# Attention scores and maxima of two heads side by side on half the array each, with a new PSUM plan, the causal score mask on GpSimd and straight-line steps

## What is computed

```
x = x + attention_a(layernorm(x))     # causal; three heads weigh a third of the tokens by 1.6
x = x + ffn(layernorm(x))
x = x + attention_b(layernorm(x))     # not causal; q and k are rotated by position
x = x + ffn(layernorm(x))

scores = einsum('bhqd,bhkd->bhqk', q, k) / sqrt(8)
out = einsum('bhqk,bhkd->bhqd', softmax(scores), v) @ w_out + bias
ffn:  h = silu(x @ w1 * s1) * (x @ w2 * s2); h = gelu(h @ h1 * s); h = gelu(h @ h2 * s); out = h @ w3 * s
```

## Time and profile before

| what | value |
|---|---|
| device time, median of 3 runs | 2662.58 us (2661.67 to 2663.25) |
| profiled execution: its span, first to last instruction | 2666.0 us |
| PE busy | 2374.0 us (89%), 15042 matmuls |
| DVE busy | 1745.9 us (65%) |
| ACT busy | 1516.8 us (57%) |
| POOL busy | 825.3 us (31%) |
| attention a, first to last weighted sum | 99.9 to 859.5 us |
| attention b, first to last weighted sum | 1374.9 to 2239.2 us |

### The profile page before, as it was taken

How to read it: one execution, slowest core, us unless ns; L and a number is a source line. 1 busy time by engine, 2 the same in 40 slices (tenths; PEclk the granted TensorE clock), 3 DMA queues, 4 the chain that set the end, 5 groups by cost and what they waited for, 6 DMA issues and landing times. The chain is left out here.

```text
span 2666.0 us, 48309 instructions
## 1 busy us (share of the span) xinstructions
PE 2374.0 (89%) x15042; PEld 1272.8 (48%) x15042; DVE 1745.9 (65%) x2625; ACT 1516.8 (57%) x2948; POOL 825.3 (31%) x933
## 2 busy tenths in 40 slices
PE   1999889889897699999489999999999995899998
PEld 0455445445442488887223323333233321688886
DVE  6766666656661576665198878787777870666663
ACT  0366556556565355555037767676676774455554
POOL 3223222222210255544322222222223300355454
PEclk9899999999998799999589999999999998999999
DMA  5334334334331000000224333332333311000000
GB/s 163 85 80 100 83 74 103 76 74 102 76 76 20 10 0 0 0 0 1 71 51 91 72 74 73 72 86 63 74 71 69 86 35 28 5 12 12 12 12 12
DMA packets 114561, 146.81 MB, mean 55 GB/s; under 512 B 27600, under 2 KB 88656, under 8 KB 113232
## 3 DMA queue, kind: packets, MB, share of 16 engines
q1 hardware_dynamic: 114384, 144.60, 23.6%
HBM read 78.47 MB, written 66.06 MB: 54 GB/s over the span
## 5 line engine op out<-in xcount | busy, mean ns | idle before, releaser
L533 DVE TENSOR_REDUCE b_negmax<-ps_max 128x2 f32<-128x1024 f32 x512 | 610.4, 1219 | 180.8 <-PE ps_max L652 180.6
L617 ACT ACTIVATE b_prob<-ps_score 128x512 f32<-128x512 f32 x1024 | 555.8, 594 | 260.9 <-PE ps_score L636 244.0
L617 ACT ACTIVATE a_prob<-ps_score 128x512 f32<-128x512 f32 (+3 forms) x1024 | 419.5, 435 | 271.9 <-PE ps_score L639 219.8
L533 DVE TENSOR_REDUCE a_negmax<-ps_max 128x2 f32<-128x256 f32 (+3 forms) x512 | 407.4, 820 | 226.9 <-PE ps_max L655 226.4
L652 PE MATMUL ps_max<-stack_k,b_stack_q 96*128 96x512 bf16 x1024 | 383.3, 395 | 33.0 <-DVE b_negmax L533 17.5
L636 PE MATMUL ps_score<-b_stack_q,stack_k 100*128 100x512 bf16 x1024 | 395.5, 389 | 18.5 <-ACT b_prob L617 17.0
L652 PE MATMUL ps_max<-stack_k,a_stack_q 96*128 96x128 bf16 (+3 forms) x1024 | 305.1, 312 | 57.1 <-DVE a_negmax L533 25.5
L636 PE MATMUL ps_score<-a_stack_q,stack_k 100*128 100x512 bf16 (+3 forms) x1024 | 319.3, 314 | 16.0 <-ACT a_prob L617 14.0
L636 PEld LDWEIGHTS ps_score<-b_stack_q,stack_k 100*128 100x128 bf16 x1024 | 99.2, 98 | 383.1 <-ACT b_prob L617 328.0
L670 PE MATMUL ps<-b_prob,b_v_aug 128*9 128x512 f32 x2048 | 272.6, 605 | 8.8 <-ACT b_o_raw L589 7.1
L945 PE MATMUL ps_score<-fb_h,w_hi 128*128 128x512 f32 x1024 | 247.4, 398 | 3.9 <-DVE fb_h L860 2.8
(11 more groups left out here) (142 smaller groups left out, 3116.1 us busy)
## 6 DMA issues: line engine op xcount, KB each, us to landing
stack_k<-d_stack SPq DMA_DIRECT2D x128, 192.0 KB, 4.0
d_stack<-a_parts SPq DMA_DIRECT2D x64, 192.0 KB, 2.8
a_stack_q<-d_stack SPq DMA_DIRECT2D x64, 192.0 KB, 3.3
d_stack<-b_parts SPq DMA_DIRECT2D x64, 192.0 KB, 2.8
b_stack_q<-d_stack SPq DMA_DIRECT2D x64, 192.0 KB, 3.7
d_stack<-a_parts SPq DMA_DIRECT2D x64, 128.0 KB, 2.8
d_stack<-b_parts SPq DMA_DIRECT2D x64, 128.0 KB, 2.8
d_stack<-a_parts SPq DMA_DIRECT2D x64, 64.0 KB, 2.5
```

Of the source, the lines that this page charges most:

```text
L533: dve.tensor_reduce(m["negmax"][:, t, :, p], m["ps_max"][:, 2 * (k % 2):2 * (k % 2) + 2, 0:keys], AX.X, ALU.max, negate=True).then_inc(s[" ...
L617: act.activation(m["prob"][u % 2][:, g, lo:S], m["ps_score"][:, g % 2, 0:S - lo], ACT.Exp)\
```

## The change

Five things change in the attention stages.

1. `stack_q` and `stack_k` hold head 0 of a pair in rows 0 to 49 and head 1 in rows 64 to 113 (`SIDE` = 64): 48 rows of products and 2 of the negated maximum. `stack_k` exists once. A score matmul has 50 contraction rows and a maximum matmul 48; the built program gives each a tile of 64 array rows by 128 columns, and the two heads of a pair stand behind each other on different row halves and write different banks.
2. The score mask matmul is gone. GpSimd instead sets the upper triangle of the diagonal block to zero in `prob` after the Exp (`mask`, line 498, 16 a step, attention a only), and `weigh` waits for it. The mask of the maxima stays on PE.
3. `prob` has 4 buffers in place of 2, and `weigh` comes two units behind its scores in place of one.
4. PSUM is dealt in turns by consumer: what ACT reads (scores, transposed maxima, transposed x) rotates over 3 banks of `ps_score`, what DVE reads (maxima, projections, output projection) over the two double banks of `ps_max`. Each use waits only for the use that had the bank before.
5. All loops in the program text are written out, in the ffn stages too, and GpSimd's work of a step is spread over its units. The reciprocal moves from unit 5 to 7, the transposed maxima of half 0 from unit 12 to 10.

```
-            def step(n, c):
+            for n in range(STEPS):
                 for u in range(UNITS):
-
-                    if on(n, 1):
-                        maxes(n - 1, 1 - c, 2 * u, 0)
-                    if on(n, 2):
-                        score(n - 2, c, u, 0)
...
+                    if on(n, 2):
+                        scores(n, u, 0)
+                    if on(n, 1):
+                        maxes(n, 2 * u)
+                    if u < 2 and on(n, 3):
+                        weigh(n - 3, UNITS - 2 + u)
+                    if u >= 2 and on(n, 2):
+                        weigh(n - 2, u - 2)
+                    if on(n, 2):
+                        scores(n, u, 1)
+                    if on(n, 1):
+                        maxes(n, 2 * u + 1)
                     misc_work(n, u)
```

```
+                for o in range(2):
+                    k = 4 * u + 2 * half + o
+                    rows = slice(SIDE * o, SIDE * o + KROWS + AUG)
+                    act_bank_free(pe, n, "score", k)
+                    pe.matmul(act_bank("score", k)[:, 0:S - lo], m["stack_k"][c][rows, p, P * j:P * (j + 1)],
+                              m["stack_q"][c][rows, p, lo:S], start=True, stop=True).then_inc(s["score"], 1)
...
+                dve_banks_free(pe, n, "max", k)
+                to, keys = dve_banks("max", k), P * (t + 1) if causal else S
+                for o in range(2):
+                    rows = slice(SIDE * o, SIDE * o + KROWS)
+                    last = pe.matmul(to[:, o, 0:keys], m["stack_q"][c][rows, p, P * t:P * (t + 1)],
+                                     m["stack_k"][c][rows, p, 0:keys], start=True, stop=True)
                 if causal:
-                    last = pe.matmul(m["ps_score"][:, g % 2, 0:P], m["mask_k"][:], m["ident_b"][:],
-                                     start=False, stop=True, skip_group_check=True)
...
+                    for o in range(2):
+                        last = pe.matmul(to[:, o, keys - P:keys], m["mask_q"][:], m["ident_b"][:],
+                                         start=False, stop=True, skip_group_check=True)
+                last.then_inc(s["max_ps"], 1)
```

```
+            def mask(b, u):
+
+                pool.wait_ge(s["prob"], count(4 * UNITS, b, 4 * u + 4))
+                at = P * (u % T)
+                tri = m["prob"][u % PROBS][:, :, at:at + P]
+                pool.affine_select(out=tri, in_=tri, compare_op=ALU.is_ge, fill=0.0, base=0,
+                                   pattern=[[0, 4], [1, P]], channel_multiplier=-1).then_inc(s["masked"], 1)
...
+    act_turns, dve_turns = [], []
+    for u in range(UNITS):
+        act_turns += [("score", 2, 4 * u + g) for g in range(4)]
+        dve_turns += [("max", 1, 2 * u), ("max", 1, 2 * u + 1)]
+        for name, lag in (("nm1", 2), ("nm0", 1), ("xT", 0)):
+            if SLOT[name] == u:
+                act_turns.append((name, lag, 0))
+        for name, lag in (("proj", 3), ("q", 0), ("qr", 0), ("k", 0), ("kr", 0), ("v", 0)):
+            if SLOT[name] == u and (rotary or name not in ("qr", "kr")):
+                dve_turns.append((name, lag, 0))
```

More of the change, by code:

```diff
@@ L173, in _ @@
             for c in range(2):
-                last = dve.memset(m["stack_k"][c][:], 0.0)
+                last = dve.memset(m["stack_k"][c][:], 1.0)
             last.then_inc(zeroed, 1)
             dve.wait_ge(zeroed, 1)
[L177 to L182, removed]
         @block.sync
@@ L256, in attention @@
     m["parts"] = sb("parts", [P, 2, 3, S], BF16)
[L257 removed]
+    m["prob"] = [sb(f"prob{c}", [P, 4, S]) for c in range(PROBS)]
     m["negmax"] = sb("negmax", [P, T, 2, PAIRS])
@@ L291, in attention @@
[L291 to L296, removed]
-        while True:
[L298 to L306, removed]
+    def on(n, lag):
+        return 0 <= n - lag < B
@@ new lines, in load @@
+            def load(b, c, h):
+                wait(sp, s["score"], count(4 * UNITS, b - 2, 2 * UNITS * (h + 1)))
+                pairs = slice(HALF * h, HALF * (h + 1))
+                for o in range(2):
+                    q, k = (m["d_stack"][i, o].rearrange("t d p n -> (t d) p n") for i in range(2))
+                    rows = slice(SIDE * o, SIDE * o + KROWS)
+                    sp.dma_start(m["stack_q"][c][rows, pairs, :], q[:, pairs, :]).then_inc(s[f"half{h}"], 16)
+                    sp.dma_start(m["stack_k"][c][rows, pairs, :], k[:, pairs, :]).then_inc(s[f"half{h}"], 16)
@@ L406, in _ @@
                         .then_inc(s["w_raw"], 16)
-            pipeline(sp, step)
+            for n in range(STEPS):
+                c = n % 2
+                if on(n, 2):
+                    aug(1, n - 2, c)
+                if on(n, 3):
+                    outputs(n - 3)
+                if on(n, 0):
+                    store(n)
+                    load(n, c, 0)
+                if on(n, 1):
+                    aug(0, n - 1, 1 - c)
+                if on(n, 0):
+                    load(n, c, 1)
         @block.gpsimd
@@ L589, in group_out @@
                 act.activation(m["o_raw"][:, G], m["ps_out"][:], ACT.Copy).then_inc(s["o_raw"], 1)
-            def step(n, c):
-                if causal and isinstance(n, int) and n == 2:
+            for n in range(STEPS):
+                if causal and n == 2:
                     act.wait_ge(s["w_rest"], len(W_PIECES))
@@ L624, in _, with scores @@
             pe.wait_ge(s["loads"], 80 if rotary else 64)
-            def score(b, c, u, g):
+            def scores(n, u, half):
+                b, c = n - 2, n % 2
                 G, j = u // T, u % T
-                p, o = 2 * G + g // 2, g % 2
-                if g == 0 and u % (UNITS // 2) == 0:
+                p, lo = 2 * G + half, width(j)
+                if half == 0 and u % (UNITS // 2) == 0:
                     h = u // (UNITS // 2)
@@ L783, in pipeline @@
         def pipeline(eng, step):
-            for n in range(3):
-                step(n)
-            with eng.Fori(3, B - 1) as n:
-                step(n)
-            for n in range(B - 1, B + 2):
+            for n in range(B + 2):
                 step(n)
```

443 lines of the change are left out of this document (217 added, 226 removed).

## The result

| | us, median | runs |
|---|---|---|
| before | 2662.9 (2661.7 to 2664.8) | 4 |
| changed | 2573.3 (2562.1 to 2578.8) | 4 |

The ratio is 0.9652, 95% interval 0.9627 to 0.9677: faster by 3.5%. The forecast was 2404 us with a range of 2300 to 2500. The sign was right, but only a third of the forecast gain came, and the time lies outside the range. The profiled execution of the changed kernel took 2562.1 us, the quickest of its four.

The account below looks back on a forecast made before the run. PE was taken to bound attention, afterwards SP's transfers in a and DVE with waits in b. Savings of 143 us in a and 115.5 in b off the 2666.0 us span, less 3.4 to the median, gave 2404 us (range 2300 to 2500).

Parts of the forecast that it names:

- A pair costs what one costs: Attention scores and maxima: two matmuls on two row halves cost one's 0.22 us, saving 14.1 us a step in b.
- Changes of the array's shape cost 0.09 us each: Attention a: about three more shape changes a unit at 0.09 us each add 4.3 us of PE a step.
- TensorE needs 33.9 us of a step of a: Attention a: PE work a step falls from 42.2 to 33.9 us.
- my bounds (37.3): PE work in a step of a: 29.6 us if shape changes cost nothing, 37.3 at 0.16 us each.
- the 36 us that I gave to a step without a ring: Attention a, steps 2 and 16, where SP has no outputs or no stores: 33.9 us and 2 for waits.
- The mask takes 0.65 us and is hidden: GpSimd in attention a: 16 masks of 0.65 us, 10.4 us a step, hidden behind the two units between scores and sums.
- b at 48 us: Attention b: a step takes 48 us, between DVE's 43.9 and the earlier 53.7, with added waits from PE's in-order issue.
- Loop edges go, straight-line code costs nothing: Attention: PE's 3.14 us "issue" idle every second step of a goes; writing out loops, ffn's too, costs nothing.
- That is 39.5 us, above PE's 33.9: Attention a: a step lasts 39.5 us, set by SP's transfers, and PE idles some 4 us.
- the ring of attention a: Landing of half 0, units 0 and 1, `aug` (5.5 us), 33.0 us of transfers, 1 us for unit 7, next landing.
- the sign that I had named: In the new profile, a step of a near 39.5 us whose first maximum waits for a load of `stack_k`.
- The second rival: Attention a at about 44 us a step, PE at 1.2 GHz after its wait, slow units lengthening the ring: 2462 us; 18%.

Follow-up runs that it names:

- the kernel with the cut ring: Changed kernel with the reciprocal at unit 6, half 0's transposed maxima at unit 9, their rows stored before its q and k loads: 2475.8 us.
- The run with the wait filled: Changed kernel with five extra fp32 matmuls ahead of TensorE's wait at the start of each step of attention a from step 2: 2533.2 us, 0.9493.

## Why the prediction was wrong

**The forecast by its steps.**

- *A pair costs what one costs*: right. Pair to pair 0.22 us at clock 1.00, and 0.45 on the same rows.
- *Changes of the array's shape cost 0.09 us each*: borne out for one unit, as a reading of starts. In the rows above the maxima of 128 columns take 0.16 us to the next instruction and their masks 0.21. By the 0.06 us for 128 columns in the earlier trace rows the pair would be 0.06 and the two masks 0.12: 0.10 and 0.09 us more, for a change of shape behind each.
- *TensorE needs 33.9 us of a step of a*: too low by up to 3.3 us. The clean step of the kernel with the cut ring lasts 39.04 us, 37.2 of them busy, which is the upper end of my bounds (37.3). Short waits for the third bank are counted as busy there, and no view tells them apart. So the 36 us that I gave to a step without a ring were too few as well.
- *The mask takes 0.65 us and is hidden*: right on both counts.
- *b at 48 us*: right in size (48.88), and wrong in its floor. I took VectorE's 43.9 us as the bound and added 4 for coupling. With VectorE's load cut by 16 us the step still takes 48.0. Of the waits that I had listed, the one for the third bank of the scores is 2.7 us a step where I had put 1.3, and the one for ScalarE's copy ahead of the first sum 0.7 where I had put 2, by the two rows of waits above.
- *Loop edges go, straight-line code costs nothing*: the edges went: no step of a begins with a wait of the cause "issue". But the rest of the span is 11.6 us longer: 3.1 us in one step of the ffn behind a, 4.7 us in that ffn's last steps, 3.1 us in steps 0 and 1 of b, and the rest in small amounts (an ffn step takes 23.51 us where it took 23.44). In that ffn the clock fell twice while PE was busy, 2 to 3 us behind a short wait. The two waits, and windows over the falls:

```profile
1061.33 4.55 PE L1020 MATMUL ps_out<-w_hi,fa_h 128*128 128x128 f32 x32 [0.60 <-POOL fa_h L849]
1229.03 4.96 PE L1020 MATMUL ps_out<-w_hi,fa_h 128*128 128x128 f32 x32 [1.02 <-POOL fa_h L849]
```

```profile
1064.00:1072.00 8.00, 8.00 (x27) 6.66 (x27) 4.65 (x14) 1.32 (x2) 1.13 (x1) 0.57 0.00 0
1230.00:1240.00 10.00, 10.00 (x43) 8.71 (x43) 4.62 (x8) 1.55 (x3) 1.02 (x1) 0.66 0.00 0
```

**The step that failed** is "That is 39.5 us, above PE's 33.9", the ring of attention a. That SP's chain closes a ring was right, and that PE would wait in it. Two of its terms were too small:

1. I let the ring end with the landing of the last load of half 0, 4.0 us after its issue. But behind these loads SP stores the rows of the maxima of half 0 and loads them again, and the first score of the next step needs those. From the last load's issue to the first score are 7.4 us: 3.4 more. For the same reason the sign that I had named, a first maximum that waits for `stack_k`, isn't what the trace shows; it is the first score that waits, for `a_stack_q<-d_nm`. This term is read from the queue's rows. No run moves the rows alone without holding up something else.
2. I let the reciprocal go out 17.9 us after the ring's start (5.5 to `aug`, 11.4 to the store of the reciprocals, 1 for unit 7). Its store came at 22.9 us (627.70 - 604.77), 5.0 more, the reciprocal itself at 22.35, since the wait had sent TensorE's clock to 0.50. The run with the wait filled moves the reciprocal to 18.4 us: 4.0 of the 5.0 are the clock, and 1.0 is missing from my sum at full clock too.

The piece between them, from that store to the last load's issue, was right: 17.15 us (644.85 - 627.70) where I had 17.56. So 5.0 and 3.4 less 0.4 are the 8.0 us between 39.5 and the 47.45 of this turn. Twelve steps, 4 to 15, at 47.3 and not 39.5 are 94 of the 118 us. Steps 2 and 3 are 4 more, and steps 16 and 17 took 90 us to the last sum where I had put 70: they end at clock 0.50:

```profile
795.00:831.00 36.00, 30.78 (x162) 6.58 (x154) 0.55 (x1) 19.73 (x53) 9.53 (x14) 0.50 0.12 26
```

The second rival named the mechanism, PE's wait at 1.2 GHz with slow units in the ring, with 18%. It was priced at 4.5 us a step, about what the clock did cost (4.0), but on a ring without the rows and with b and the rest as forecast, and so ended at 2462, still 111 us short. The mechanism was to be read in the earlier trace rows: behind a wait of 2.81 us the sums ran slow there. What I wrote as forecast, a wait of 4 us a step at full clock, left that row out. Whoever forecasts a wait of TensorE at every step has to forecast the clock behind it too.

## What to carry to other kernels

Where an engine gets enough faster for a chain of transfers to bound, write the chain down as a closed ring, instruction by instruction in each queue's order, until it is back at the instruction it began with; what stands last in the in-order queue is easily left out. If TensorE waits in the ring, its work behind the wait may run at the lower clock and may itself lie in the ring, as here for 12 us behind 4.8; price it at 1.2 GHz. Then look for the one instruction whose place is free: here moving the reciprocal by two units was worth 74 us by the medians, where the whole change brought 90.

## What was not expected of the hardware

- The granted clock stayed at 0.50 through all steps of attention b (PE busy 100.00 of 100 us) in the kernel whose pairs used one row half only, and was 1.00 in steps 3 to 15 of b in the same code with two halves.
- In ffn, which is the same code as before but for the loop, one step of 23.5 us took 26.66 in the changed kernel, with some 7 us at 0.50 behind a wait of only 0.60 us. The same wait, 0.58 to 0.60 us, stands in the other steps of this ffn without a fall, and one of 0.49 to 0.59 us in the steps of the kernel before. A wait of 1.02 us was followed by a fall in the changed kernel (at 1229 us) and by none in the kernel before (at 1252 us). What decides between the two, no run shows.
- After a wait of 1.10 us of TensorE for VectorE (with the reciprocal at unit 5) the clock was 0.50 for 3.4 us; after one of 4.80 us (the changed kernel), for 12 us. Both times TensorE had gone back to work at once.
